# Attention scores from two 64-row products of halved fp32r operands, changed to one 99- or 102-row product of three bf16 parts

## The chip, the cores and the metric

One NeuronCore of a Trainium2 chip runs the whole program. The metric is device time in microseconds; lower is better. Times of the kernel before are three runs on one chip, and one further execution was recorded by the hardware profiler.

## What is computed

The reference is a stack of eight residual blocks on x[4, 512, 256]. Two of them are softmax attentions with 16 heads of 16 dimensions, and only these are touched:

```python
# block 1 (causal, with a bias that depends on head and key)
scores = einsum('bqhd,bkhd->bhqk', q, k) * scale + bias[None, :, None, :]
scores = where(causal, scores, -1e9)
p = softmax(scores, axis=-1); ctx = einsum('bhqk,bkhd->bqhd', p, v)
x = x + ctx @ Wout.T + b_out
# block 5 (no mask; rotary position on q and k; 4 key/value heads, repeated 4 times)
scores = einsum('bhqd,bhkd->bhqk', Qr, Kr) / HEAD_DIM ** 0.5
weights = softmax(scores, axis=-1); out = einsum('bhqk,bhkd->bhqd', weights, V_rep)
x = x + out @ W_o
```

The other six blocks are two expert feed-forwards, one attention over features, two sparse feed-forwards and a scan.

## The kernel before, in words

`stages` runs the blocks one behind the other. `attention` is called twice: "attn0" is block 1 (`causal` true), "attn1" is block 5. x stays in the on-chip memory for the whole program.

One attention has B = 4 sequences and 16 heads. Four heads make a unit, a unit has NT = 4 steps, one for each tile of 128 queries, so there are 64 steps, 16 for each sequence, and 15 more in which the pipeline empties or the last jobs run. The table `at` lists, for every step t, jobs for its middle and for its end. Each engine walks the same table, in the same order, and does the jobs that are its own. Nothing else orders the work: an engine goes through its list strictly in turn, and semaphores make it wait for the others.

A step has two halves of two heads each. In each half TensorE (PE) does, in this order:

- `scores1` (L940) of step t: the queries of one tile against keys, into banks 0 to 3 of PSUM, only for the row maxima. In attn0 the width is 128, 256, 384 or 512 keys for t mod 4 = 0, 1, 2, 3; in attn1 always 512.
- `scores2` (L964) of step t - 7: the transposed product, keys against queries, with the maxima as an extra row, into banks 4 and 5. Its widths in attn0 are 384, 256, 128, 512.
- in attn0 `masks1` (L950) and `masks2` (L973), which add the causal mask by products with an identity in bf16, 128 columns each.
- after the first half, the jobs of the step's middle.

After both halves come `context` (L988) of step t - 8, which multiplies probabilities with values for four heads side by side (128 rows, 32 columns, fp32), and the jobs of the step's end.

VectorE (DVE) takes the maximum over each half's scores (`row_max`, L1312), and ScalarE (ACT) the exponentials (L1160), one for each head. `scores1` of a half waits until the maximum of the half before last is taken, and `scores2` of a head waits until the exponential two heads earlier has emptied its bank.

**How a product of scores is made.** A number is cut into a high and a low fp32r part. A head's 16 dimensions are stacked three times (high·high, low·high, high·low), 48 rows; rows 48 and 49 carry the bias in attn0, row 63 the maximum, the rest are zeros. Heads lie in pairs: the even one in partitions 0 to 63 and the odd one in 64 to 127 of `qs` and `ks`, so that the two products of a half use the upper and the lower 64 rows of the array. `qs` and `ks` have two buffers, for alternating sequences.

**How the stacks are filled.** For each chunk (128 query or key rows, "q0", "k0", "q1", and in attn0 "k1") ACT writes the high part and DVE (attn0, and the first sequence of attn1) or GpSimd (POOL) the low part. Then SP's queue copies them into the stack, six DMAs a chunk (`stacks`, L828). Before the first of these the queue writes constants into the stacks: zeros (L850), ones (L843) and the bias (L868). The maxima of a unit go from `negm` through a PE transpose (L996, job `maxima`, in the middle of step 4u + 4) and an ACT copy to `mT`, and by two DMAs into the stack (L836). PE waits for them before step 4u + 7.

**Other jobs.** "rows" (L899) transposes the normalised x, "project" (L915) makes a chunk (in attn1 as "plain" in the middle and "swapped" at the end of a step), "values" (L928), "flip" (L1002) and "merge" (L1009) transpose results, "out" (L1018) is the last product. All of these and `maxima` use bank 7 (`MISC`), in the order of the table: PE may begin a job only when the job before it in that bank has been copied out by its engine. The first sequence's jobs ("early") run before step 0. After its early jobs DVE computes the norm statistics of the other three sequences (L119 to L1331), and only then takes the first row maximum.

## Time and profile before

| | us |
|---|---|
| median of three runs | 1644.63 (1636.43 to 1647.76) |
| profiled execution, its own time | 1641.78 |
| span of its trace | 1639.7 |
| attn0: first score product to last | 46.0 to 318 |
| attn1: first score product on | from 888.1 |

| engine | busy us (share) |
|---|---|
| PE | 1398.7 (85%) |
| PE weight loads | 1002.1 (61%) |
| DVE | 1049.0 (64%) |
| ACT | 625.2 (38%) |
| POOL | 295.8 (18%) |

The trace gives start and duration of each instruction, and for a gap the event that ended it. Ends of matmuls are modelled, so a busy PE is no proof of a PE at its limit; the distance between starts tells more. The engines run in turn through fixed lists, so the time of a stage is that of a chain that goes from engine to engine, and it is read from the starts.

### The profile page before, as it was taken

The page shows a single profiled execution, that of the slowest core. Times are in us where ns is not written, and L with a number is a line of the kernel's source. Part 1 is how long each engine was busy: PE and PEld are TensorE (multiplying, and loading weights), DVE is VectorE, ACT ScalarE, POOL GpSimd, SP SyncE. Part 2 cuts the span into 40 slices and gives each one's busy share as a digit, 9 for nine tenths or more (in the row PEclk, how much of TensorE's full clock was granted, in tenths as well). Part 3 has the DMA queues.
Part 4 walks back from the last instruction along what each step waited for, and adds up shares of the span by engine and source line. Part 5 has one row for each costly group of instructions (what it writes and reads, how often), then busy time and mean ns, then how long its engine had stood idle before and what let it go on. Part 6 is the DMA issues. An engine that isn't in the chain of part 4 may idle for free. (4 is left out here: it accounts for less than half of the span.)

```text
span 1639.7 us, 21649 instructions
## 1 busy us (share of the span) xinstructions
PE 1398.7 (85%) x8144; PEld 1002.1 (61%) x8144; DVE 1049.0 (64%) x2056; ACT 625.2 (38%) x1160; POOL 295.8 (18%) x251
## 2 busy tenths in 40 slices
PE   3799999857999877799976899898879979889897
PEld 2455555446888766688864444343257767677676
DVE  5555555187887456778746556666256568888775
ACT  1254544342333212333321455656632323433321
POOL 0210000044433200243331320200040200120010
PEclk9799999578999988999996799999989989999899
DMA  8615220040000000000015404110000000000000
GB/s 190 87 27 79 44 37 2 1 149 1 1 1 1 1 0 1 0 1 1 1 39 73 75 27 75 27 24 1 1 0 1 1 1 1 0 1 1 13 13 26
DMA packets 23063, 42.00 MB, mean 26 GB/s; under 512 B 4705, under 2 KB 6497, under 8 KB 22833
## 3 DMA queue, kind: packets, MB, share of 16 engines
q1 hardware_dynamic: 22960, 40.64, 13.2%
q8 instruction: 64, 1.05, 0.3%
q14 instruction: 39, 0.31, 0.1%
HBM read 14.54 MB, written 2.10 MB: 10 GB/s over the span
## 5 line engine op out<-in xcount | busy, mean ns | idle before, releaser
L1312 DVE TENSOR_REDUCE attn_negm<-ps 128x2 f32<-128x1024 f32 (+3 forms) x256 | 256.2, 1021 | 115.5 <-PE ps L940 57.4
L1160 ACT ACTIVATE attn_probs<-ps 128x512 f32<-128x512 f32 (+3 forms) x512 | 237.0, 515 | 188.9 <-PE ps L973 112.0
L480 POOL TENSOR_TENSOR moe_h_low<-moe_h,moe_h_high 128x512 fp32r<-128x512 f32 x96 | 139.8, 1458 | 328.8 <-ACT moe_h_high L430 328.8
L964 PE MATMUL ps<-attn_qs,attn_ks 64*128 64x512 f32 (+3 forms) x512 | 154.9, 418 | 38.1 <-ACT attn_probs L1160 35.4
L447 ACT ACTIVATE moe_silu<-ps 128x512 f32<-128x512 f32 x96 | 57.4, 598 | 228.0 <-PE ps L353 227.9
L940 PE MATMUL ps<-attn_ks,attn_qs 63*128 63x512 f32 (+3 forms) x512 | 120.9, 469 | 26.6 <-DMA attn_ks<-attn_part_low 21.5
L964 PEld LDWEIGHTS ps<-attn_qs,attn_ks 64*128 64x128 f32 x512 | 72.1, 193 | 102.7 <-ACT attn_probs L1160 97.9
L1683 PE MATMUL ps<-sb_f_down,tail_h 128*128 128x256 f32 x512 | 123.3, 387 | 7.1 <-DVEq L1976 7.1
L988 PE MATMUL ps<-attn_probs,attn_va 128*32 128x512 f32 (+3 forms) x1024 | 123.8, 559 | 0.0
L1683 PEld LDWEIGHTS ps<-sb_f_down,tail_h 128*128 128x128 f32 x512 | 98.5, 193 | 24.0 <-DVEq L1976 7.3
L940 PEld LDWEIGHTS ps<-attn_ks,attn_qs 63*128 63x128 f32 x512 | 51.9, 199 | 93.8 <-issue 62.4
L1949 DVE TENSOR_TENSOR tail_h<-tail_silu,ps 128x512 f32<-128x512 f32 x64 | 43.5, 682 | 89.0 <-PE ps L1673 56.9
L1789 ACT ACTIVATE tail_silu<-ps 128x512 f32<-128x512 f32 x64 | 38.1, 596 | 113.8 <-PE ps L1667 113.8
L503 DVE TENSOR_TENSOR moe_h<-moe_silu,ps 128x512 f32<-128x512 f32 x64 | 43.4, 686 | 56.7 <-PE ps L360 39.0
L382 PE MATMUL ps<-f_down_high,moe_h_high 128*128 128x256 f32 x256 | 73.9, 289 | 3.7 <-POOL moe_h_low L480 3.7
L382 PE MATMUL ps<-f_down_high,moe_h_low 128*128 128x256 f32 x256 | 72.6, 283 | 0.0
L382 PE MATMUL ps<-f_down_low,moe_h_high 128*128 128x256 f32 x256 | 72.1, 282 | 0.0
L430 ACT ACTIVATE moe_h_high<-moe_h 128x512 fp32r<-128x512 f32 x96 | 60.0, 625 | 29.7 <-DVE moe_h L503 29.1
L1667 PE MATMUL ps<-tail_xh,tail_gate_high 128*128 128x512 f32 x128 | 63.8, 498 | 2.9 <-POOL tail_up_low L1824 2.9
L1277 DVE RECIPROCAL attn_rden<-ps 128x16 f32<-128x16 f32 x32 | 8.2, 258 | 89.7 <-PE ps L1002 89.7
L1958 DVE TENSOR_TENSOR tail_ge<-tail_mag 128x1536 bf16<-128x1536 f32 (+2 forms) x48 | 55.8, 1218 | 0.7 <-ACT tail_mag L1777 0.7
L973 PE MATMUL ps<-sb_a_mask_kq,sb_identb 64*128 64x128 bf16 x512 | 52.8, 227 | 0.0
(319 smaller groups left out, 3281.2 us busy)
## 6 DMA issues: line engine op xcount, KB each, us to landing
attn_qs<-attn_part_high SPq DMA_DIRECT2D x64, 128.0 KB, 4.9
attn_qs<-attn_part_low SPq DMA_DIRECT2D x32, 128.0 KB, 4.5
attn_ks<-attn_part_high SPq DMA_DIRECT2D x32, 128.0 KB, 6.1
attn_ks<-attn_part_low SPq DMA_DIRECT2D x16, 128.0 KB, 7.0
out_x<-x SPq DMA_DIRECT2D x4, 512.0 KB, 2.6
x<-in_x SPq DMA_DIRECT2D x1, 1536.0 KB, 12.9
attn_qs<-attn_mT SPq DMA_DIRECT2D x64, 4.0 KB
moe_raw<-in_f_gate SPq DMA_DIRECT2D x2, 512.0 KB, 6.3
```

What stands on the lines that cost most here:

```text
L382: last = pe.matmul(ps[:, bank + t // 2, (t % 2) * D:(t % 2 + 1) * D], hp[:, j % RING, t * P:(t + 1) * P], wp[:, jw, :], start=j == 0 and t ...
L430: act.activation(hc.high[:, n % RING, :], h[:, n % RING, :], ACT.Copy).then_inc(high_done, 1)
L447: act.activation(sg[:, j % 2, :], ps[:, 2 * (j % 2), :], ACT.Silu).then_inc(silu_done, 1)
L480: pool.tensor_tensor(hc.low[:, j % RING, :], h[:, j % RING, :], hc.high[:, j % RING, :], ALU.subtract).then_inc(low_done, 1)
L940: last = pe.matmul(ps[:, 2 * (n % 2) + k, 0:width1(qt)], qs[e:e + ROWS1, b % 2, hd // 2, qt * P:(qt + 1) * P], ks[e:e + ROWS1, b % 2, key_ ...
L964: last = pe.matmul(ps[:, SC + k, 0:width2(kt)], ks[e:e + ROWS2, b % 2, key_tile(hd), kt * P:(kt + 1) * P], qs[e:e + ROWS2, b % 2, hd // 2, ...
L988: last = pe.matmul(ps[SLOT * j:SLOT * (j + 1), CTX, T - width2(kt):T], va[:, b % 2, kt, hd % KH, :], pr[:, s3 % RING, j, 0:width2(kt)], st ...
L1160: act.activation(pr[:, s2 % RING, j, 0:n], ps[:, SC + k, 0:n], ACT.Exp, scale=HD ** -0.5).then_inc(exp_done, 1)
L1312: dve.tensor_reduce(m, ps[:, 2 * half:2 * half + 2, 0:width1(qt)], AX, ALU.max, negate=True).then_inc(r1_free, 1)
L1667: last = pe.matmul(ps[:, bank, :], wp[:, c, j * P:(j + 1) * P], xp[:, p % 2, c, :], start=c == 0 and k == 0, stop=c == DC - 1 and k == 2)
L1683: last = pe.matmul(ps[:, DOWN + t // 2, (t % 2) * D:(t % 2 + 1) * D], h[:, j, t * P:(t + 1) * P], w_down[:, j, :], start=j == 0 and t % 2 ...
L1958: c.do(dve.tensor_tensor(ge[:, first:first + n, :], mag[:, lo, :].unsqueeze(1).broadcast_to([P, n, T]), mag[:, lo + 1:4, :], ALU.is_ge))
```

## The change

- The parts are bf16 and there are three of each number. A head has six products of 16 dimensions stacked (96 rows), then three rows of bias in attn0, then three rows of maximum: 99 or 96 rows for `scores1`, 102 or 99 for `scores2`. A head uses all 128 partitions; no two heads are paired. The number of score matmuls and their columns stay.
- A mask is one product over 128 rows where it was two over 64: two instructions for a half where there were four.
- No zero rows. Bias comes in three bf16 parts from the host.
- attn0: after DVE has taken the rest (`rest`, L1226 in the changed kernel), POOL makes parts two and three (L1161, L1163), and the copies wait for these. attn1: three subtractions or casts instead of one, on DVE for the first sequence (`low0`), on POOL for the others.
- The maxima are cut into three parts by four small DVE instructions (`split_maxima`, L1312 to L1315) behind the last `row_max` of a unit. PE turns the 48 columns in one bf16 product (L965), ACT copies 48 rows, one DMA loads them. The job moves from the middle of step 4u + 4 to that of 4u + 5.
- Each stack DMA moves as many bytes as before (128 KB), as 128 rows of 1 KB where it was 64 of 2 KB.

```diff
-DATA = 48
+DATA = 96
+PARTS = 3
...
-    MROW = P // 2 - 1
-    ROWS1, ROWS2 = MROW, MROW + 1
+    ROWS1 = DATA + (PARTS if causal else 0)
+    ROWS2 = ROWS1 + PARTS
...
-        at[4 * u + 4][0].insert(0, ("maxima", u))
+        at[4 * u + 5][0].insert(0, ("maxima", u))
...
-                if causal:
-                    sp.wait_ge(free["dve"], jobs.count[("project", b, ch, "plain")])
-                else:
-                    sp.wait_ge(low_ready, NCH * b + k + 1)
+                sp.wait_ge(low_ready, NCH * b + k + 1)
...
+                order = (0, 0, 1, 0, 1, 2) if ch[0] == "q" else (0, 1, 0, 2, 1, 0)
+                for r, which in enumerate(order):
+                    sp.dma_start(dst[16 * r:16 * r + 16, b % 2, first:first + n, :],
+                                 part[which][0:rows_of[ch], k, :]).then_inc(stack_loaded[int(ch[1])], 16)
...
-            zero_rows(ks)
-            zero_rows(qs)
-            ones_rows(ks, MROW, 1)
+            ones_rows(ks, ROWS1)
             if causal:
-                ones_rows(qs, DATA, 2)
-                sp.wait_ge(const_ready, 2)
+                ones_rows(qs, DATA)
+                sp.wait_ge(first_in, FIRST)
...
-                    e = 64 * k
-                    last = pe.matmul(ps[:, 2 * (n % 2) + k, 0:width1(qt)], qs[e:e + ROWS1, b % 2, hd // 2, qt * P:(qt + 1) * P],
-                                     ks[e:e + ROWS1, b % 2, key_tile(hd), 0:width1(qt)], start=True, stop=True)
+                    last = pe.matmul(ps[:, 2 * (n % 2) + k, 0:width1(qt)], qs[0:ROWS1, b % 2, hd, qt * P:(qt + 1) * P],
+                                     ks[0:ROWS1, b % 2, hd % KH, 0:width1(qt)], start=True, stop=True)
...
-                for c in range(2):
-                    for k in range(2):
-                        last = pe.matmul(ps[:, 2 * (n % 2) + k, qt * P:(qt + 1) * P], identb[64 * k:64 * k + 64, c, :],
-                                         w["mask_qk"][64 * k:64 * k + 64, c, :], start=False, stop=c == 1, skip_group_check=True)
-                        if c == 1:
-                            last.then_inc(r1_ready, 1)
+                for k in range(2):
+                    pe.matmul(ps[:, 2 * (n % 2) + k, qt * P:(qt + 1) * P], identb[:, :], w["mask_qk"][:, :],
+                              start=False, stop=True, skip_group_check=True).then_inc(r1_ready, 1)
...
+            def split_rest(b, ch):
+                k, n = CHUNKS.index(ch), rows_of[ch]
+                done = (1 if causal else 2) * (NCH * b + k + 1)
+                pool.tensor_copy(part[1][0:n, k, :], rest[0:n, k, :]).then_inc(rest_steps, 1)
+                pool.wait_ge(rest_steps, done)
+                pool.tensor_tensor(part[2][0:n, k, :], rest[0:n, k, :], part[1][0:n, k, :], ALU.subtract).then_inc(low_ready, 1)
...
+            def split_maxima(u):
+                if u >= 2:
+                    dve.wait_ge(ready, jobs.number[("maxima", u - 2)])
+                dve.wait_ge(r1_free, 2 * NT * (u + 1))
+                m, parts = negm[:, u % 2, :], mparts[:, u % 2, :]
+                cm.start(u)
+                cm.step(dve.tensor_copy(parts[:, 0:16], m))
+                cm.step(dve.tensor_tensor(mrest[:, :], m, parts[:, 0:16], ALU.subtract))
+                cm.step(dve.tensor_copy(parts[:, 16:32], mrest[:, :]))
+                dve.tensor_tensor(parts[:, 32:48], mrest[:, :], parts[:, 16:32], ALU.subtract).then_inc(m_split, 1)
```

**PE at the end of step 32 and the beginning of step 33 of attn1**, where a chunk of the last sequence is projected. Before (L940, L964 scores, L996 maxima, L988 context, L1002 flip, L915 the six products of a projection):

```order
L964 MATMUL ps<-attn_qs,attn_ks 128x512 x2
L996 MATMUL ps<-sb_ident,attn_negm 16x128
L940 MATMUL ps<-attn_ks,attn_qs 128x512 x2
L964 MATMUL ps<-attn_qs,attn_ks 128x512 x2
L988 MATMUL ps<-attn_probs,attn_va 32x512 x4
L1002 MATMUL ps<-sb_ident,attn_ctxs 128x128 x4
L940 MATMUL ps<-attn_ks,attn_qs 128x512 x2
L964 MATMUL ps<-attn_qs,attn_ks 128x512 x2
L915 MATMUL ps<-attn_xh,attn_wq_high 128x512
```

And now, from the first half of step 33 on (L916, L936 scores, L965 maxima, L892 projection, L957 context):

```order
L916 MATMUL ps<-attn_ks,attn_qs 128x512 x2
L936 MATMUL ps<-attn_qs,attn_ks 128x512 x2
L965 MATMUL ps<-sb_identb,attn_mparts 48x128
L892 MATMUL ps<-attn_xh,attn_wq_high 128x512
L892 MATMUL ps<-attn_xl,attn_wq_high 128x512
L892 MATMUL ps<-attn_xh,attn_wq_low 128x512
```

The maxima stood a step earlier, with a flip between them and the projection; now they stand directly ahead of the projection, and both use bank 7.

**SP's queue ahead of the first stack copies of attn0.** Before:

```order
L856 DMA x<-in_x 128x3072
L850 DMA attn_ks<-attn_zeros 13x8x512 x4
L850 DMA attn_qs<-attn_zeros 13x8x512 x4
L843 DMA attn_ks<-attn_ones 1x8x512 x4
L843 DMA attn_qs<-attn_ones 2x8x512 x4
L868 DMA attn_ks<-attn_bias_high 1x8x512 x4
L868 DMA attn_ks<-attn_bias_low 1x8x512 x4
```

Now:

```order
L837 DMA x<-in_x 128x3072
L832 DMA attn_ks<-attn_ones 3x16x512 x2
L832 DMA attn_qs<-attn_ones 3x16x512 x2
L845 DMA attn_ks<-sb_a_bias 1x16x512 x6
L821 DMA attn_qs<-attn_part 16x8x512 x6
L821 DMA attn_ks<-attn_part 16x8x512 x6
```

Twenty-four copies of constants become ten, and the eight of zeros, 208 KB each, are gone.

## Rows read from the trace of the kernel before

**Rows 1.** Waits, 46 to 331 us (attn0): engine line, awaited; us in total, times, longest.

```profile
ACT attn_probs L1160 <- PE ps L973: 112.0, 112, 3.3
...
PEld ps L964 <- ACT attn_probs L1160: 36.0, 84, 1.2
```

**Rows 2.** Busy time by stretch: start:end, length, busy (x count), PEclk, DMA share, GB/s.

```profile
46.00:102.00 56.00, 49.59 (x438) 30.80 (x438) 32.26 (x43) 20.00 (x48) 7.57 (x8) 0.83 0.48 68
```

**Rows 3.** Timeline, step 61 of attn1: start, us, engine, line, xcount, [idle before, releaser].

```profile
1152.30 0.50 PE L940 MATMUL ps<-attn_ks,attn_qs 63*128 63x512 f32 x2
1152.64 0.40 PE L964 MATMUL ps<-attn_qs,attn_ks 64*128 64x512 f32 x2
1153.13 1.08 ACT L1160 ACTIVATE attn_probs<-ps 128x512 f32<-128x512 f32 x2 [1.64 <-PE ps L964]
1153.78 0.98 PE L964 MATMUL ps<-attn_qs,attn_ks 64*128 64x512 f32 x2 [0.51 <-ACT attn_probs L1160]
...
1154.70 1.07 PE L988 MATMUL ps<-attn_probs,attn_va 128*32 128x512 f32 x8
1155.69 0.49 PE L940 MATMUL ps<-attn_ks,attn_qs 63*128 63x512 f32 x2
```

**Rows 4.** Timeline, step 55 of attn0, second half.

```profile
258.52 0.18 PEld L964 LDWEIGHTS ps<-attn_qs,attn_ks 64*128 64x128 f32 x1 [0.31 <-ACT attn_probs L1160]
258.52 0.11 PEld L950 LDWEIGHTS ps<-sb_a_mask_qk,sb_identb 64*128 64x128 bf16 x2
...
259.31 0.60 ACT L1160 ACTIVATE attn_probs<-ps 128x512 f32<-128x512 f32 x1 [0.84 <-PE ps L973]
```

**Rows 5.** Timeline, the beginning of attn0.

```profile
7.31 4.67 SPq L850 DMA_DIRECT2D attn_ks<-attn_zeros  x4
...
19.74 0.63 ACT L1148 ACTIVATE attn_wv_high<-sb_a_wv 128x512 fp32r<-128x512 f32 x1 [10.95 <-DMA x<-in_x]
...
24.38 2.64 SPq L868 DMA_DIRECT2D attn_ks<-attn_bias_low  x4
...
34.25 4.00 DVE L119 BATCH_NORM_STATS2 attn_stats<-x 128x6 f32<-128x256 f32 x12
...
41.69 0.17 DVE L130 SCALAR_TENSOR_TENSOR attn_rstd<-attn_newton,attn_rstd 128x12 f32<-128x12 f32 x1
41.89 0.17 DVE L1331 TENSOR_SCALAR attn_minus<-attn_mv 128x12 f32<-128x12 f32 x1
...
46.03 0.47 PE L940 MATMUL ps<-attn_ks,attn_qs 63*128 63x128 f32 x2 [12.43 <-DMA attn_ks<-attn_part_low]
```

**Rows 6.** The page's DMA issues over the program: count, KB each, us to landing.

```profile
attn_qs<-attn_part_high SPq DMA_DIRECT2D x64, 128.0 KB, 4.9
...
x<-in_x SPq DMA_DIRECT2D x1, 1536.0 KB, 12.9
```

**Rows 7.** Timeline, the beginning of attn1.

```profile
880.45 0.69 DVE L1269 TENSOR_TENSOR attn_part_low<-attn_qk,attn_part_high 128x512 fp32r<-128x512 f32 x1 [0.70 <-ACT attn_part_high L1096]
881.05 4.00 DVE L119 BATCH_NORM_STATS2 attn_stats<-x 128x6 f32<-128x256 f32 x12
...
888.94 1.23 DVE L1312 TENSOR_REDUCE attn_negm<-ps 128x2 f32<-128x1024 f32 x1 [0.16 <-PE ps L940]
```

**Rows 8.** Timeline, a projection's last product in attn1 and the scores behind it.

```profile
1035.63 0.40 PE L915 MATMUL ps<-attn_xh,attn_wq_low 128*128 128x512 f32 x1
1035.95 0.19 PEld L940 LDWEIGHTS ps<-attn_ks,attn_qs 63*128 63x128 f32 x2 [0.36 <-issue]
```

**Rows 9.** Timeline, step 8 of attn0: maxima, their copy, a projection.

```profile
71.22 0.27 PE L996 MATMUL ps<-sb_ident,attn_negm 128*16 128x128 f32 x1
71.85 0.25 ACT L1111 ACTIVATE attn_mT<-ps 16x128 fp32r<-16x128 f32 x1
...
72.20 0.59 PE L915 MATMUL ps<-attn_xh,attn_wk_high 128*128 128x512 f32 x1 [0.71 <-ACT attn_mT L1111]
```

**Rows 10.** Timeline, one subtraction on POOL in attn1.

```profile
1049.61 1.27 POOL L1187 TENSOR_TENSOR attn_part_low<-attn_qk,attn_part_high 128x512 fp32r<-128x512 f32 x1
```

More of the change, by code:

```diff
@@ L754, in attention @@
         cut = {n: Halves(s.sb(n + "_high", w[n].shape, F32R), s.sb(n + "_low", w[n].shape, F32R)) for n in names}
-        part = Halves(s.sb("part_high", [P, NCH, T], F32R), s.sb("part_low", [P, NCH, T], F32R))
-        qs, ks = s.sb("qs", [P, 2, HEADS // 2, T], F32R), s.sb("ks", [P, 2, KT, T], F32R)
-        ones = s.sb("ones", [HEADS, T], F32R)
-        zeros = s.sb("zeros", [P, T], F32R)
-        if causal:
-            bias = Halves(s.sb("bias_high", [HEADS, T], F32R), s.sb("bias_low", [HEADS, T], F32R))
-        else:
+        part = [s.sb(f"part{r}", [P, NCH, T], BF16) for r in range(PARTS)]
+        qs, ks = s.sb("qs", [P, 2, HEADS, T], BF16), s.sb("ks", [P, 2, KH, T], BF16)
+        ones = s.sb("ones", [PARTS * HEADS, T], BF16)
+        rest = s.sb("rest", [P, NCH, T])
+        if not causal:
             qk, rot = s.sb("qk", [P, NCH, T]), s.sb("rot", [P, 2, T])
@@ L1084, in project @@
                     act.wait_ge(ready, jobs.number[job])
-                    act.activation(part.high[0:n, k, :], ps[0:n, jobs.bank[job], :], ACT.Identity,
+                    act.activation(part[0][0:n, k, :], ps[0:n, jobs.bank[job], :], ACT.Identity,
                                    bias=w["bqk"][0:n, k:k + 1]).then_inc(high_ready, 1)
@@ L1095, in high @@
                 act.wait_ge(turned, NCH * b + k + 1)
-                act.activation(part.high[0:n, k, :], qk[0:n, k, :], ACT.Copy).then_inc(high_ready, 1)
+                act.activation(part[0][0:n, k, :], qk[0:n, k, :], ACT.Copy).then_inc(high_ready, 1)
             def values(b, v):
@@ L1205, in _ @@
                     turn(0, job[2])
+                if causal and job[0] == "project":
+                    projected(0, job[2])
             normalise(1)
@@ L1214, in _ @@
                             turn(job[1], job[2])
+                        if causal and job[0] == "project":
+                            projected(job[1], job[2])
                         if job[0] == "high":
@@ L1335, in _ @@
                         row_max(2 * t + half)
+                        if half == 1 and t % NT == NT - 1:
+                            split_maxima(t // NT)
                     for job in todo:
@@ L2091, in bf16_bits, with bf16_parts @@
     return (bits >> 16).astype(np.uint16)
[L2094 to L2096 removed]
 def head_rows(heads):
[L2101 removed]
+    return np.array([HD * h + d for d in range(HD) for h in range(heads)])
+def bf16_parts(v):
+    parts = []
+    for _ in range(PARTS):
+        parts.append(bf16_bits(v))
+        v = v - (parts[-1].astype(np.uint32) << 16).view(np.float32)
+    return np.concatenate(parts)
 def shape_constants():
```

133 lines of the change are left out of this document (56 added, 77 removed).

## The prediction

> **What bounds the kernel now.** I read the views in this order. The busy shares do not decide: PE is busy 85%, but with modelled ends. The chain that ended last lies in the last third, which the change leaves alone; so I read the two attentions for themselves: their waits first, then the timeline of single steps, then the place where each attention begins.
>
> The waits of attn0 name no single full engine: ACT waits 112.0 us for PE's masks, and PE's weight loads wait 36.0 us for ACT's exponentials [rows 1]. The two wait for each other in turn; what counts is the length of that ring. One plain step of attn1 shows it [rows 3]: scores1 at 1152.30, scores2 at 1152.64, its two exponentials from 1153.13 to 1154.21, the second half's scores2 from 1153.78, because head by head they wait for these exponentials, then the context at 1154.70, and the next step at 1155.69. The step is 3.39 us. Of it the first half's products up to the first exponential are 0.83, the exponentials and the loads behind them 1.1, the second half's last product until the context 0.4, the context 0.99. The second half's scores1 lies beside the exponentials and costs nothing. In attn0 the same ring holds the masks too [rows 4]: the second head's weight load starts at 258.52, the next exponential at 259.31, 0.79 us later.
>
> What begins attn0 is a transfer: PE's first score product waits until 46.03 for the copies into the stack, 12.43 us after its last early product [rows 5]. Ahead of the stack copies SP's queue issues constants until 27.02, and the early projections themselves start late, because ACT waits for x's 1.5 MB until 19.74 [rows 5]. DVE is close behind as the bound: its statistics run from 34.25 to 42.06. In attn1 DVE is the bound at the beginning: statistics from 881.05, first maximum at 888.94 [rows 7].
>
> **The change, part by part.** The sum is made against the profiled execution, 1641.78 us.
>
> *Products in turn.* Before, two heads' products share a slot: 0.34 us from the first pair to the next, 0.11 of it exposed weight load and 0.23 the 512 columns [rows 3]. Now two heads stand one behind the other. For bf16 columns I take the same 0.23 at most; four of 512 columns take 0.05 + 4 x 0.22 = 0.93 where two pairs took 0.57. The first exponential needs only the third of the four, so it starts 0.15 later. The load for bf16 weights is shorter: two masks' loads fit in 0.11 where one fp32r load takes 0.18 [rows 4]. That gives back 0.05 on the last product of the second half. So a step of attn1 gets 0.09 longer, 64 x 0.09 = **+5.8**. In attn0 one mask of 128 rows takes the slot of a pair of 64, and where the heads are apart (second half) four masks stand in the ring and not eight: the 0.79 of rows 4 become about 0.65. The 16 steps with 512 columns in both products (t mod 4 = 3) gain this and lose 0.22 in front: +0.1 each. The 48 narrower ones lose little in front: -0.1 each. Together 1.6 - 4.8 = **-3.2**. The seven emptying steps of each attention have no scores1 and gain 0.1: **-1.5**.
>
> *No switch between 64 and 128 rows.* After a projection of 128 rows the next scores1 loads its weights 0.32 us after the start of the last product, whose 512 columns take 0.23: 0.09 of a gap, and the load's 0.11 is exposed [rows 8]. With all in 128 rows both should go. Jobs at a step's end: 16 flips, 8 merges, 8 outs, 6 rows in each attention and 9 swapped projections in attn1, 85 in all, each with one switch on the ring: 85 x 0.2 = **-17**. The context, 32 columns wide, still switches twice a step.
>
> *Steps that wait for nothing.* In 12 steps of attn1 and 18 of attn0 a projection or a values job stands in the middle; the exponentials are over when PE returns, and every column counts. Attn1: four pairs x 0.22 = 0.88 more, less two switches of 0.2 and 0.1 of loads, about +0.35; attn0, with 320 columns in the mean, +0.1: **+6**.
>
> *Maxima a step later.* Directly ahead of a projection in the same bank, they make PE wait until ACT has copied them, and ACT does this behind the half's two exponentials. The one place that has this order now is step 8 of attn0: product at 71.22, copy at 71.85, projection at 72.20, 0.71 us waited [rows 9]. In the new order this is so in steps 5, 17, 21, 33, 37 of attn0 and 5, 17, 33 of attn1; in the two steps 5 ACT has no exponentials yet. From rows 3 the wait would be 1.4 in attn1 (exponentials end 1.9 into the step, the copy takes 0.25, PE is there at 0.9). I take 1.0 x 6, less 1.0 for step 8: **+5**. For the deadline, step 4u + 7, more than one step of 2.4 us or longer is left after the copy, and one DMA of this kind takes under 2.
>
> *DVE's four small instructions.* 0.20 from start to start [rows 5], 0.85 a unit. They lie between the last maximum of a unit and the next step's first, where DVE waits anyway. In the first steps, where DVE is the bound, they count: **+0.9** in attn1, **+0.5** in attn0.
>
> *Beginning of attn0.* Eight copies of zeros (1.66 MB) and six others go. I assume that x then lands 4.7 us earlier: 512 KB take 2.6 us to write, 1536 KB would take 8 by that, and take 12.9 beside the zeros [rows 6]. All early work moves with it, DVE's statistics end at 37.4. The stack copies lose the wait for SP's queue and gain two POOL instructions, 1.27 us each by the nearest row [rows 10]; by that the twelve copies that step 0 needs are issued by 32 and landed, at 4.9 us each [rows 6], by 38. Taken: **-8**. Bounds: -11, if nothing but x counts, and 0, if landing is unchanged.
>
> *Beginning of attn1.* DVE makes three parts instead of two for three chunks: a cast (0.4) and a subtraction of 0.69 [rows 7] with two waits, 1.25 each, all ahead of the statistics: +3.8, less 0.5 for the memset of zeros: **+3.3**. Other POOL work (the same cuts for later sequences) has 16 steps of cover, 50 us for 5 us.
>
> Sum: 5.8 - 3.2 - 1.5 - 17 + 6 + 5 + 1.4 - 8 + 3.3 = -8.2, so 1633.6. The median of three stands 2.9 above the profiled execution, so on its scale 1636. I forecast **1635**.
>
> **Rivals.** *A, faster, 1620.* In 46 to 102 us PE's clock was granted at 0.83 [rows 2], that is 19 us at 1.2 GHz and the rest at 2.4 GHz, behind the long wait. With a shorter wait and more columns in flight it may stay high: half of these 19 us, and the same again in attn1's first stretch. 15 us in the best case, under 1635. Against it: the wait before step 0 does not vanish, and PE had waits of this kind before.
>
> *B, slower, 1665.* PE becomes the bound. 256 pairs of 512 columns (0.23) and 256 of 320 in the mean (0.14) are 59 + 36 = 95 us of streaming that comes on top, and my sum exposes only 12. It decides as soon as the second half's scores1 ends after the first exponential: by rows 3 at 1.38 against 1.58 us into the step, 0.2 of margin. If every step goes over and a third is exposed, +32. For it: the margin is small, and in attn0 the narrow exponentials leave less. Against it: the ring has 1.1 us of exponentials in each step. The Trainium skill (TensorEngine Tiling (Array Packing), Theoretical Speedup) gives products of at most 64 rows up to a doubling by tiles, which this change gives up; by that rule alone all 95 would show and the time be 1730. Rows 3 speak against: PE's score products wait for ACT there.
>
> *C, the copies, 1645.* A copy is now 128 rows of 1 KB. If the time goes by rows and not by bytes, the twelve copies ahead of step 0 take twice as long (19 instead of 9.6 us at one each 0.8, 46 - 27 us for 24), the beginning of attn0 gains nothing (+8), and that of attn1 loses some us more. No row has 1 KB between on-chip places. The Trainium skill (DMA: Bandwidth & Descriptors, Specifications) puts the minimum for full rate at 512 B; by it C would be out, and no row here shows it.
>
> *D, no effect of the missing switch, 1648.* If the 0.2 of rows 8 belongs to the scores' first load in any mode, -17 shrinks to -4.
>
> **How the numbers follow.** Forecast 0.50, A 0.20, B 0.10, C 0.10, D 0.10. About 1% (16.4 us) is what a measurement of this kernel can tell from no change. Faster by more, under 1628.2: A nearly whole and the lower edge of the forecast, 0.27. Slower by more, over 1661.1: B's larger part, 0.08. Within: 0.65. The range 1619 to 1650 takes in A's centre, C and D, and leaves B and A's far side out.
>
> **What would show it.** Right: the first score product of attn0 at 36 to 40 us; plain steps of attn1 3.45 to 3.5 us apart; scores right behind a flip with no gap; steps 17 and 33 longer by 0.5 to 1.4 us; attn1's first maximum about 3.5 us later behind its block's beginning. Wrong: PE's weight loads of scores2 no longer waiting for exponentials (B); the first product still at 44 or later (C); PE's clock at 1.0 throughout (A).

## The result, and the profile after

| | before | after | ratio of after to before |
|---|---|---|---|
| median of four runs of each, us | 1643.55 | 1624.41 (1616.93 to 1629.84) | 0.9857 [0.9813, 0.9902] |
| once more, six runs of the change, us | 1643.61 | 1622.26 | 0.986 [0.9822, 0.9898] |
| profiled execution, span, us | 1639.7 | 1617.3 | |
| second profile of each, span, us | 1645.2 | 1616.9 | |

The change is 1.4% faster, inside the forecast's range and beyond its 1%. The kernel's time varies with the clock that PE is granted, and one profile is not enough for that, so both kernels were profiled twice. The table gives the stages, each from one start of a PE product to the next ("loop": from the first product of `scores1` to the last; "emptying": from there to the last product of `out`; the last products of `scores2` lie in it):

| stage, us | before | before, 2nd | after | after, 2nd | mean change |
|---|---|---|---|---|---|
| up to attn0's first score product | 46.0 | 44.3 | 40.1 | 41.0 | -4.6 |
| loop of attn0 | 241.3 | 251.7 | 236.5 | 236.0 | -10.3 |
| emptying of attn0 | 43.4 | 43.5 | 32.5 | 31.9 | -11.3 |
| from there to attn1's first score product | 557.3 | 552.4 | 553.0 | 552.8 | -2.0 |
| loop of attn1 | 271.6 | 272.5 | 277.2 | 277.1 | +5.1 |
| the rest | 480.0 | 480.8 | 478.1 | 478.2 | -2.2 |

The profiles differ by 25.3 us, the medians by only 19 and 21. Of the 25.3 us, 4.7 lie in stages of other blocks, which the change leaves alone (2.2 in the last row, 2.5 between attn0 and the beginning of attn1).

attn1, which shares all the products' changes, got slower. The gain lies in attn0's loop and emptying. The table by stretches says why. Its columns are start:end, length, busy time (x count) of PE, PE's weight loads, DVE, ACT and POOL, then PE's granted clock, DMA share and GB/s. Before, first profile (attn0's loop, its emptying, attn1's loop):

```profile
46.03:287.31 241.28, 222.88 (x2188) 133.56 (x2189) 129.74 (x182) 109.05 (x276) 12.04 (x12) 0.94 0.31 43
287.31:330.80 43.49, 35.90 (x213) 18.30 (x207) 5.19 (x9) 15.04 (x38) 0.00 (x0) 0.61 0.00 1
888.10:1159.70 271.60, 243.35 (x1265) 107.69 (x1265) 170.56 (x178) 149.39 (x286) 40.65 (x39) 0.94 0.21 37
```

Before, second profile, attn0's loop and emptying:

```profile
44.30:296.00 251.70, 234.65 (x2189) 140.15 (x2189) 129.81 (x182) 109.04 (x276) 13.20 (x12) 0.88 0.29 42
296.00:339.50 43.50, 35.77 (x212) 18.32 (x205) 5.19 (x9) 15.15 (x38) 0.00 (x0) 0.61 0.00 1
```

After, the same three stretches:

```profile
40.11:276.60 236.49, 214.35 (x1709) 123.05 (x1709) 143.07 (x243) 108.99 (x277) 34.93 (x37) 0.96 0.36 49
276.60:309.10 32.50, 24.47 (x173) 11.68 (x171) 5.75 (x13) 15.15 (x38) 0.00 (x0) 0.89 0.01 1
862.10:1139.20 277.10, 254.32 (x1264) 98.35 (x1265) 187.79 (x253) 149.04 (x287) 55.41 (x57) 0.94 0.22 36
```

The clock has two levels, 1.2 and 2.4 GHz, so a stretch of length L at a granted clock c spent 2 x (1 - c) x L at the lower one. In attn0's loop that is, summed unrounded, 29.8 and 61.1 us before, 17.1 and 12.4 after; in the emptying 34.1 and 34.1 before, 6.8 and 3.4 after. The two profiles of before give the price: 10.4 us more for 31.3 us more at 1.2 GHz, **0.33 us for each us at the lower clock**, with the same instructions. (Between the runs over 65 and 96 rows below it is 12.4 us for 31.0, or 0.40.) In the changed kernel no stretch at 1.2 GHz lies between 60 and 280 us, in either profile; before had 3 in the first profile (72, 134, 202 us) and 5 in the second (71 to 273 us).

The steps can also be compared directly. Where a step ran wholly at 2.4 GHz in a profile of each kernel, its shortest times are set side by side: 54 of the 63 steps of attn0's loop are together 0.6 us longer after the change, 53 of attn1's 1.3 us longer. So the instructions gained nothing in the sum.

The single step has hardly changed. Timeline of step 61 of attn1 after (start, us, engine, line, xcount, [idle before, releaser]), to be laid beside [rows 3]:

```profile
1131.39 0.60 PE L916 MATMUL ps<-attn_ks,attn_qs 96*128 96x512 bf16 x2
...
1131.83 0.59 PE L936 MATMUL ps<-attn_qs,attn_ks 99*128 99x512 bf16 x2
...
1132.30 1.09 ACT L1127 ACTIVATE attn_probs<-ps 128x512 f32<-128x512 f32 x2 [1.63 <-PE ps L936]
...
1133.44 0.10 PEld L936 LDWEIGHTS ps<-attn_qs,attn_ks 99*128 99x128 bf16 x1 [0.39 <-ACT attn_probs L1127]
...
1134.76 0.39 PE L916 MATMUL ps<-attn_ks,attn_qs 96*128 96x512 bf16 x1
```

The first exponential comes 0.91 us into the step (before 0.83), and from the last `scores2` to the next step it is 1.32 us (before 1.42): 3.37 us for 3.39. Steps with a flip went from 3.98 to 3.87, those with a projection in the middle from 5.66 to 5.87 and 7.16 to 7.37. In attn0 the widest steps (t mod 4 = 3) grew from 3.22 to 3.35 and plain narrow ones fell from 2.40 to 2.34. So the ring of PE and ACT is the same one; PE's weight loads still wait for the exponentials (after, 40 to 309 us of the trace, to be compared with [rows 1]):

```profile
ACT attn_probs L1127 <- PE ps L944: 100.0, 110, 3.1
PEld ps L936 <- ACT attn_probs L1127: 43.4, 100, 0.9
```

What got longer is the step with the maxima right ahead of a projection. Step 33 of attn1, 8.57 us, before 7.13:

```profile
1011.50 1.09 ACT L1127 ACTIVATE attn_probs<-ps 128x512 f32<-128x512 f32 x2 [1.64 <-PE ps L936]
...
1011.57 0.24 PE L965 MATMUL ps<-sb_identb,attn_mparts 128*48 128x128 bf16 x1
1012.47 0.26 ACT L1080 ACTIVATE attn_mT<-ps 48x128 bf16<-48x128 f32 x1
...
1012.83 0.47 PE L892 MATMUL ps<-attn_xh,attn_wq_high 128*128 128x512 f32 x1 [1.03 <-issue]
...
1014.06 0.40 PE L892 MATMUL ps<-attn_xh,attn_wq_low 128*128 128x512 f32 x1
1014.30 0.12 PEld L916 LDWEIGHTS ps<-attn_ks,attn_qs 96*128 96x128 bf16 x2 [0.27 <-issue]
```

PE stands for 1.03 us until ACT, behind two exponentials, has emptied the bank. The last two rows answer to [rows 8]: the load now comes 0.24 us after the product's start, not 0.32.

One more wait grew, at the beginning of step 11 of attn1, where PE needs the second unit's maxima. Before:

```profile
934.00 0.19 PEld L940 LDWEIGHTS ps<-attn_ks,attn_qs 63*128 63x128 f32 x2 [3.34 <-DMA attn_qs<-attn_mT]
```

After:

```profile
904.11 3.73 SPq L821 DMA_DIRECT2D attn_ks<-attn_part  x6
...
908.53 0.78 SPq L827 DMA_DIRECT2D attn_qs<-attn_mT  x1
...
912.46 0.13 PEld L916 LDWEIGHTS ps<-attn_ks,attn_qs 96*128 96x128 bf16 x2 [5.65 <-DMA attn_qs<-attn_mT]
```

PE turned these maxima at 899.4, but their DMA stands in SP's queue behind stack copies and is issued at 908.53. Step 10 takes 10.71 and 10.42 us, before 8.19 and 8.34; with POOL's instructions shortened and the maxima a step earlier (e6_short_pool below) it takes 7.56. Two steps later PE runs at the higher clock where before it did not, so steps 10 to 13 together grew by only 0.3 to 0.5 us.

The beginning of attn0, to be compared with [rows 5]:

```profile
16.53 0.63 ACT L1115 ACTIVATE attn_wv_high<-sb_a_wv 128x512 fp32r<-128x512 f32 x1 [8.37 <-DMA x<-in_x]
...
25.62 3.83 SPq L821 DMA_DIRECT2D attn_qs<-attn_part  x6
...
37.80 0.17 DVE L1331 TENSOR_SCALAR attn_minus<-attn_mv 128x12 f32<-128x12 f32 x1
...
40.12 0.37 PE L916 MATMUL ps<-attn_ks,attn_qs 99*128 99x128 bf16 x2 [10.53 <-DMA attn_ks<-attn_part]
```

x lands at 16.5 (before 19.7), the copies are issued from 25.6 (before 27.1), and yet PE waits until 40.1. The DMA view tells why: packets, MB and rate while the stacks are filled, after (28 to 40 us) and before (30 to 39 us).

```profile
DMA packets 1749, 1.59 MB, mean 133 GB/s; under 512 B 193, under 2 KB 1749, under 8 KB 1749
```

```profile
DMA packets 930, 1.51 MB, mean 168 GB/s; under 512 B 193, under 2 KB 193, under 8 KB 930
```

All 16 DMA engines are busy in both. In these two stretches a packet of 1 KB takes 0.134 us in the mean where one of 2 KB took 0.201: the copies land 1.01 us apart, before 0.86. Yet before waited longer, because its last signal came late: eleven of the twelve copies were there at 39.3 us, the last one only at 45.9.

The beginning of attn1, against [rows 7]:

```profile
856.34 0.43 DVE L1257 CAST attn_part<-attn_rest 128x512 bf16<-128x512 f32 x1
856.80 0.69 DVE L1259 TENSOR_TENSOR attn_part<-attn_rest,attn_part 128x512 bf16<-128x512 f32 x1
857.41 4.01 DVE L119 BATCH_NORM_STATS2 attn_stats<-x 128x6 f32<-128x256 f32 x12
...
865.06 2.35 DVE L1302 TENSOR_REDUCE attn_negm<-ps 128x2 f32<-128x1024 f32 x2
```

From the last product of the block ahead to the first maximum it is 40.7 us, before 38.7 and 37.4. To the first score product it is 37.7, before 37.9 and 36.5: most of this loss lies inside the "loop of attn1", whose step 0 takes 4.3 us in place of 2.1, because DVE comes later to its first maximum.

### The profile page after: what moved, and what is told of

Read it like the earlier page. It is cut to its first block and busy times, and to the rows that moved or that the text cites. A ratio compares the mean times of both kernels' runs of the same rounds, so it can differ in the third digit from the quotient of the medians.

```text
span 1617.3 us, 20802 instructions
## 1 busy us (share of the span) xinstructions
PE 1384.7 (86%) x7632; PEld 970.3 (60%) x7632; DVE 1073.8 (66%) x2187; ACT 623.9 (39%) x1159; POOL 346.3 (21%) x301
## 5 line engine op out<-in xcount | busy, mean ns | idle before, releaser
L936 PE MATMUL ps<-attn_qs,attn_ks 99*128 99x512 bf16 (+4 forms) x512 | 153.6, 347 | 30.7 <-ACT attn_probs L1127 18.9
L916 PE MATMUL ps<-attn_ks,attn_qs 96*128 96x512 bf16 (+4 forms) x512 | 142.4, 362 | 31.0 <-DMA attn_ks<-attn_part 20.9
L936 PEld LDWEIGHTS ps<-attn_qs,attn_ks 102*128 102x128 bf16 (+1 forms) x512 | 49.1, 97 | 126.9 <-ACT attn_probs L1127 100.5
L957 PE MATMUL ps<-attn_probs,attn_va 128*32 128x512 f32 (+3 forms) x1024 | 118.3, 535 | 0.0
L916 PEld LDWEIGHTS ps<-attn_ks,attn_qs 99*128 99x128 bf16 (+1 forms) x512 | 40.1, 101 | 91.6 <-issue 46.8
L503 DVE TENSOR_TENSOR moe_h<-moe_silu,ps 128x512 f32<-128x512 f32 x64 | 43.4, 687 | 60.3 <-PE ps L360 39.6
L1669 PE MATMUL ps<-tail_xl,tail_gate_high 128*128 128x512 f32 x128 | 52.5, 410 | 0.0
```

Source lines behind the costliest of these rows:

```text
L916: last = pe.matmul(ps[:, 2 * (n % 2) + k, 0:width1(qt)], qs[0:ROWS1, b % 2, hd, qt * P:(qt + 1) * P], ks[0:ROWS1, b % 2, hd % KH, 0:width1 ...
L936: last = pe.matmul(ps[:, SC + k, 0:width2(kt)], ks[0:ROWS2, b % 2, hd % KH, kt * P:(kt + 1) * P], qs[0:ROWS2, b % 2, hd, T - width2(kt):T] ...
L957: last = pe.matmul(ps[SLOT * j:SLOT * (j + 1), CTX, T - width2(kt):T], va[:, b % 2, kt, hd % KH, :], pr[:, s3 % RING, j, 0:width2(kt)], st ...
L1669: last = pe.matmul(ps[:, bank, :], wp[:, c, j * P:(j + 1) * P], xp[:, p % 2, c, :], start=c == 0 and k == 0, stop=c == DC - 1 and k == 2)
```

## The experiments

**Does the clock's place belong to the kernel?** Second profiles of both (before2 and after2, unchanged code).

> The kernel before once more, for a second profile. Theory: stretches at 1.2 GHz again in steps 8, 24, 25 and 40 of attn0 (72, 134 and 202 us) and while attn0 empties (304 to 328 us). Rival 'chance': other places, and the emptying of attn0 at full clock, so that most of the 10.5 us that it saved in the profiles is no part of the change's worth.

> The changed kernel once more, for a closer ratio and a second profile. Theory 'clock by the work in hand': the stretches at 1.2 GHz come at the same places as in its first profile (33 to 57, 289 to 296, 313 to 330 us, nothing between 60 and 285). Rival 'chance': others, with some between 60 and 285 us. Ratio to the kernel before 0.984 to 0.990.

Measured: after2 1622.26 us, before2 1647.16 in its one run; the stages stand above. The places of the kernel before differed between its profiles (only about 72 and 200 us came back), but it had 3 and 5 stretches within 60 to 280 us, the change none; and the emptying was at 1.2 GHz for 34 us both times. "Chance" is right for the single place and wrong for the sum: the whole-program clock was 0.909 to 0.930 in all runs of the kernel before, and 0.931 to 0.942 in all ten of the change.

**What giving up the pairs costs** (e1_serial).

```diff
-                    e = 64 * k
+                    e = 0
...
-  identb[64 * k:64 * k + 64, c, :], w["mask_qk"][64 * k:64 * k + 64, c, :]
+  identb[0:64, c, :], w["mask_qk"][0:64, c, :]
```

> The kernel before, in which both heads of a pair use rows 0 to 63 of the array (and the masks too), so that their products stand one behind the other as in the change; nothing else differs (the odd head's scores are those of the even one). It tells what giving up the pairs costs by itself, and what it does to PE's clock. My forecast's step: an attn1 plain step grows from 3.39 to 3.5 us, attn0 by a few us, in all about +10, ratio 1.006. Theory 'clock' (more columns in flight keep PE's clock high in attn0 and in its emptying steps): the half-clock stretches of the kernel before at 72, 134, 202 and 304 to 328 us are gone, and the time is equal or lower than before, ratio 0.99 to 1.00. Rival 'PE bound': plain steps of 3.7 us or more, ratio over 1.015.

Measured: 1766.58 us, ratio 1.0709 [1.0639, 1.078], far from every theory. A plain step of attn1 takes 3.61 us (with 3.39 before), so there the steps' own part is 64 x 0.22 = 14 us of 120. In attn0, where the masks stand in turn too, a plain narrow step at full clock takes 3.08 us for 2.40, and the 27 steps that run at full clock in both kernels are 0.81 longer in the mean; for all 63 that would be 51 us, an estimate. attn0's loop took 337 us, PE was busy 332 of them, and the granted clock was 0.76. So the theory "clock" falls: more columns in flight did not keep the clock up. The rival "PE bound" is out for attn1, whose step stays under its 3.7, and fits attn0.

**The 64-row mode and the rows** (e3_rows64, e9_rows65, e10_rows96): the changed kernel's score products over fewer rows of the same stacks, the columns unchanged.

```diff
-  qs[0:ROWS1, b % 2, hd, ...], ks[0:ROWS1, b % 2, hd % KH, ...]
+  qs[0:64, b % 2, hd, ...], ks[0:64, b % 2, hd % KH, ...]     (65, 96; scores2 likewise)
```

All three leave bias and maxima out of the scores, and the first two other parts of the sum as well.

> The changed kernel with score products over 64 rows of the stacks only (the rest of the sum, bias and maxima are left out of the scores), so that scores are in 64-row mode again, one head behind the other; all else is the same. It isolates the switch between 64 and 128 rows. If the switch costs 0.2 us a time: flip steps of attn1 4.07 and plain ones 3.38, outs 5.4, in all some 10 to 17 us more than the changed kernel. If it costs nothing and the gain came from shorter weight loads: the same time within 3 us. Clock: if it goes by columns, the clock's stretches are those of the changed kernel; if by rows in use, they are those of the kernel before.

> As e3_rows64, with one row more: products over 65 rows, so that the array is in 128-row mode while hardly more rows are in use. Against e3_rows64 (1669 us; attn0's loop 272.2 us, 76.8 of it at half clock; flip steps of attn1 3.96) it tells whether the mode or the rows in use made that time. Theory 'mode': no switches, flip steps 3.87, and attn0's loop 236 us with 10 to 20 us at half clock, as in the changed kernel; time 1622 to 1628. Theory 'rows in use': flip steps 3.87 too, but attn0's loop keeps 40 to 70 us at half clock and takes 245 to 260 us; time 1635 to 1655.

> Control for the two runs over 64 and 65 rows, whose scores lack bias and maximum so that the exponentials overflow: products over rows 0 to 95, that lack the same, with nearly all rows of the change in use. If those values have no part in it, time and clock are the changed kernel's: 1618 to 1628 us, attn0's loop 236 us with 10 to 20 us at half clock. If the values themselves move the clock, it stands near e3_rows64 or e9_rows65 instead.

| rows | median us | ratio to before | attn0's loop us | its clock | flip step of attn1 |
|---|---|---|---|---|---|
| 64 | 1669.45 | 1.0146 [1.0107, 1.0186] | 272.3 | 0.86 | 3.96 |
| 65 | 1642.29 | 0.9973 [0.9937, 1.0009] | 248.7 | 0.90 | 3.87 |
| 96 | 1624.66 | 0.9854 [0.9779, 0.993] | 236.3 | 0.96 | 3.87 |
| 99 and 102 (after2) | 1622.26 | 0.986 [0.9822, 0.9898] | 236.0 | 0.97 | 3.87 |

The rows by stretches of e3_rows64, attn0's loop and attn1's:

```profile
41.50:313.80 272.30, 257.91 (x1709) 121.23 (x1709) 145.21 (x243) 109.76 (x277) 35.72 (x38) 0.86 0.31 42
...
902.70:1191.10 288.40, 267.50 (x1265) 98.04 (x1265) 188.02 (x255) 148.96 (x287) 55.34 (x57) 0.91 0.22 35
```

e9_rows65:

```profile
40.80:289.50 248.70, 227.36 (x1708) 128.81 (x1709) 143.27 (x243) 108.95 (x276) 35.30 (x37) 0.90 0.34 46
...
880.60:1162.10 281.50, 258.68 (x1265) 99.72 (x1265) 187.86 (x254) 149.06 (x287) 55.41 (x57) 0.93 0.22 35
```

e10_rows96:

```profile
41.10:277.40 236.30, 214.31 (x1709) 123.08 (x1709) 143.00 (x243) 108.97 (x277) 35.21 (x37) 0.96 0.36 49
```

From 65 to 96 rows the steps that run at full clock do not differ (plain 3.37 and 3.38, flip 3.87, step 17 of attn1 8.57 in both; 97 steps of the two loops together 0.4 us), so the 17.6 us between the medians go by the clock. The clock of a stage comes from one profile each, and the two profiles of before alone lay as far apart (29.8 and 61.1 us at 1.2 GHz) as these two (48.6 and 17.6). What carries the reading is that all runs agree: ten over 65 rows took 1636 to 1650 us at whole-program clocks of 0.915 to 0.927, four over 96 rows 1620 to 1631 at 0.934 to 0.938. So the theory "rows in use" forecast e9_rows65 rightly.

From 64 to 65 rows more than the rows changes. The masks of the change use 128 rows, so over 64 rows every step of attn0 has changes of mode between scores and masks. That fits its plain narrow step, 2.54 us at full clock, over 65 rows 2.33. e3_rows64 came out 45 to 47 us above the change and not 10 to 17, and its stretches at 1.2 GHz are neither those of the change nor those of before: 76.9 us in attn0's loop.

The run over 96 rows lacks bias and maxima like the other two and has the change's time, so their absence plays no part. This is the central result: at equal columns, the granted clock of attn0's loop was 0.90 with 65 rows and 0.96 with 96; over 64 rows, with the switches besides, it was 0.86.

The switch itself is read at full clock, from a flip's first product to the scores behind it. e3_rows64:

```profile
1182.64 0.66 PE L971 MATMUL ps<-sb_ident,attn_ctxs 128*128 128x128 f32 x4
...
1183.22 0.11 PEld L916 LDWEIGHTS ps<-attn_ks,attn_qs 64*128 64x128 bf16 x2 [0.17 <-issue]
1183.22 0.60 PE L916 MATMUL ps<-attn_ks,attn_qs 64*128 64x512 bf16 x2
```

The changed kernel, a flip of the same sequence:

```profile
1112.78 0.66 PE L971 MATMUL ps<-sb_ident,attn_ctxs 128*128 128x128 f32 x4
...
1113.17 0.21 PEld L916 LDWEIGHTS ps<-attn_ks,attn_qs 96*128 96x128 bf16 x2
1113.28 0.60 PE L916 MATMUL ps<-attn_ks,attn_qs 96*128 96x512 bf16 x2
```

0.58 us against 0.50; the whole flip step is 0.09 longer. Steps of attn1 with a projection in the middle, two switches, were 0.19 to 0.28 longer over 64 rows than over 65. A switch on the chain costs 0.09 to 0.14 us. The Trainium skill (TensorEngine Tiling (Array Packing), Tiling Modes) says that a change of mode drains the engine; the trace shows the delay, at this price, and not the draining itself.

**The emptying by the clock alone** (e8_filled_tail): the kernel before, with PE given work there.

```diff
+                if s1 == STEPS:
+                    pe.wait_ge(r1_free, 2 * STEPS)
...
+                    elif s2 < STEPS:
+                        filler(half)      # scores1 of the last step again, two products, unread
```

> The kernel before, with scores1's products of the last step issued again, unread, in the seven emptying steps of each attention, so that PE has in them the products of a full step. The emptying of attn0 took 43.4 and 43.5 us in the two profiles, 34.1 us of it at half clock; in the changed kernel 31.9 to 32.5 with 3.4 to 6.8. If the clock alone makes that difference, the filled emptying has under 15 us at half clock and takes 34 to 38 us, attn1's stays, 5 to 9 us less than the kernel before. Rival: the change's emptying steps are shorter by themselves (no switch, other products): the clock stays high, but 40 us or more remain; or the added products only lengthen the steps.

```profile
289.00:324.50 35.50, 29.36 (x240) 15.30 (x235) 5.18 (x9) 15.15 (x38) 0.00 (x0) 0.95 0.00 1
```

The emptying of attn0 fell from 43.5 to 35.5 us with added work, at a clock of 0.95: the clock makes at least 8 of the 11.3 us. At 0.37 us for each us at 1.2 GHz (worked out below) the emptying of before would take 32 us at the change's clock, so the remaining 3 are more likely the filler's own cost; no run separates them. The 11.3 us themselves are at the upper end of what the change gives. The emptying took 32.1 us in e4_zeros, but 36.3 in e10_rows96 and 35.5 to 38.4 in the four versions that moved the job of the last maxima, which lies in it (e2, e5, e6, e7), with 12 to 24 us at 1.2 GHz. The whole was 1647.9 us, ratio 1.0018 [0.9984, 1.0052]: the 8 us don't show. In the profile the stages outside attn0 were longer by 2 to 7 us up to attn1 and by 3 behind its loop, where the filler also runs; what of it the filler causes wasn't separated.

**The place of the maxima** (e2_maxima4, e5_mixed, e6_short_pool).

```diff
-        at[4 * u + 5][0].insert(0, ("maxima", u))
+        at[4 * u + 4][0].insert(0, ("maxima", u))                       # e2, e6
+        at[4 * u + (4 if u % 4 == 3 else 5)][0].insert(0, ("maxima", u))   # e5
```

> The changed kernel with the job maxima back in the middle of step 4u + 4. If the later place makes PE wait for ACT's copy ahead of a projection (as I forecast), steps 17, 33 of attn1 fall from 8.57 to about 7.2 us and steps 5, 17, 33 of attn0 by 0.8 each, but step 8 of each gets its old wait back: 4 to 6 us less than the changed kernel in all. Rival: the longer path over DVE's four small instructions makes PE wait at 4u + 4 for the parts, and every fourth step grows by 0.3 to 0.8 us: 30 units, 10 us more.

Measured: 1631.57 us, ratio 0.9875 [0.9811, 0.994], in its profile 14.6 us longer than the change's. Steps 17 and 33 of attn1 fell to 7.35 and 7.33, those of attn0 to 4.77, as forecast. But steps 8, 20 and 36 of attn0 rose from 6.17, 4.40 and 4.40 to 11.99, 7.38 and 6.97, and PE's clock fell at each (69, 120, 188 us), which it did not in the change. attn0's loop is 9 us longer than the change's and its emptying 5 to 6. Its timeline at step 8:

```profile
65.94 2.34 POOL L1182 TENSOR_TENSOR x<-x,sb_a_bo 128x1024 f32<-128x1024 f32 x1
66.17 2.13 DVE L1312 CAST attn_mparts<-attn_negm 128x16 bf16<-128x16 f32 x1
...
68.91 1.17 POOL L1163 TENSOR_TENSOR attn_part<-attn_rest,attn_part 128x512 bf16<-128x512 f32 x1
69.10 1.01 DVE L1315 TENSOR_TENSOR attn_mparts<-attn_mrest,attn_mparts 128x16 bf16<-128x16 f32 x1
...
70.25 0.27 PE L965 MATMUL ps<-sb_identb,attn_mparts 128*48 128x128 bf16 x1 [4.05 <-DVE attn_mparts L1315]
```

DVE's instructions on 16 columns, 0.17 us elsewhere, last until POOL's instruction ends (68.28 and 68.30; 70.08 and 70.11). In the changed kernel they do so too (2.16 us at 65.58), but there PE asks for the parts a step later. So the rival of this run, in a form that neither theory had, is right.

> As e2_maxima4 (the changed kernel with the job maxima at 4u + 4), but POOL's two instructions a chunk that make parts two and three work on 8 of 512 columns (the scores lack most of these parts). In e2_maxima4 DVE's small instructions at steps 8 and 20 ended just when POOL's ended (2.16 us beside the 2.34 us of L1182, 0.80 beside L1163, alone 0.17). If they are locked out by POOL's work: step 20 falls from 7.4 to about 4.5 us, step 8 keeps the 2.2 us beside L1182 but loses the later ones, attn0's first score product comes 1 to 2 us earlier. Rival: DVE's length there has another cause, steps 8 and 20 stay at 12 and 7 us.

```diff
-                pool.tensor_copy(part[1][0:n, k, :], rest[0:n, k, :])
+                pool.tensor_copy(part[1][0:n, k, 0:8], rest[0:n, k, 0:8])     (the subtraction likewise)
```

Measured: 1623.28 us, ratio 0.9865 [0.9817, 0.9914]. Step 20 fell from 7.38 to 4.78, step 8 from 11.99 to 8.75. Step 36 still took 6.09, with no DVE instruction held and 2.9 us of it at 1.2 GHz. At step 8 what is left of the hold is again POOL's biased add:

```profile
63.96 2.35 POOL L1186 TENSOR_TENSOR x<-x,sb_a_bo 128x1024 f32<-128x1024 f32 x1
...
65.58 0.75 DVE L1316 CAST attn_mparts<-attn_negm 128x16 bf16<-128x16 f32 x1
```

The cast begins 1.6 us into the add and ends with it (66.33 and 66.31). The first score product came 0.6 us earlier than in e2, not 1 to 2; PE still waits 9.5 us there for the copies (in e2_maxima4 10.3). The Trainium skill (SBUF — State Buffer, SBUF: two separate sides) describes an exclusive lock of a port pair that DVE and GpSimd share, by which the later one waits for the whole instruction; the trace agrees.

> The changed kernel with the job maxima back in the middle of step 4u + 4 for the last unit of each sequence alone (there no projection and no work of POOL is near), and at 4u + 5 for the others. Steps 17, 33 of attn0 go from 5.53 to 4.77 us, those of attn1 from 8.57 to 7.35, steps 16, 32, 48 get 0.1 to 0.2 longer; steps 8, 20, 36 of attn0 stay as in the changed kernel. 3 to 4 us less than the changed kernel, ratio to it 0.998. Rival: PE's clock falls somewhere else for it and the gain isn't seen.

Measured: 1618.01 us, ratio 0.9835 [0.9798, 0.9873], against 1622.26 for after2 on the same chip: 4.2 us less, as forecast. In the profile attn1's loop is 2.3 us shorter (274.8), attn0's 0.5 to 1.0, but the emptying of attn0 is 3 us longer, and the span, 1617.0, is no shorter than the change's. The intervals of the two ratios overlap. What is sure is that steps 17 and 33 take 4.78 us (attn0) and 7.33 (attn1) in place of 5.53 and 8.57. Its median is the lowest here.

**The zeros** (e4_zeros).

```diff
+            if causal:
...
+                            sp.dma_start(dst[102 + 13 * part_:115 + 13 * part_, buf, :, :],
+                                         zeros[0:104, :].unsqueeze(1).broadcast_to([104, 2, T])).then_inc(const_loaded, 16)
```

These are eight DMAs of 208 KB, into rows 102 to 127 of `ks` and `qs`.

> The changed kernel with attn0's eight fills of 208 KB of zeros issued again at the same place, into rows 102 to 127 that nobody reads (in pieces of 1 KB, before it was 2 KB). My forecast says that they cost the beginning: x lands at 19 to 20 instead of 16.5 us, the first score product comes 4 to 8 us later than 40.1, the time grows by 4 to 8 us. Rival: the beginning is bound by the stack copies alone (12 at 1.02 us), which start later only if x does, and the straggling last copy of the kernel before has another cause: first score product under 42.

Measured: 1628.52 us, ratio 0.9876 [0.9813, 0.994], 4 to 6 us above the change. x lands at 19.9, the first score product is at 46.76, 5.7 to 6.6 us later; attn0's loop is 234.6. The fills account for the whole gain at the beginning. They also bring back the late signal, which answers this run's rival: eleven copies are there at 42.2 us and the last at 46.6.

**PE kept at work in the waits** (e7_warm): e5_mixed with 36 unread products ahead of each step 0.

```diff
+            for k in range(36):
+                pe.matmul(ps[:, k % 2, :], cut["wq"].high[:, 0, 0:P], xT.high[:, 0, :], start=True, stop=True)
```

> e5_mixed, and in each attention 36 products of 128 rows and 512 columns into banks 0 and 1, which nobody reads, between the early jobs and step 0, where PE otherwise waits 10.8 us for the copies into the stacks. They compute nothing of the result. At full clock they take 36 x 0.22 = 8 us and fit into the wait. If PE's idleness there is why the first steps of both attentions run at 1.2 GHz (33 to 57 and 852 to 883 us), both stretches get shorter by 10 to 20 us; in the loops a us at half clock cost 0.33 us (before and its second profile: 29.8 and 61.1 us at half clock, 241.3 and 251.7 us long), so 6 to 12 us less than e5_mixed, ratio to it 0.993 to 0.996. Rival: the clock falls all the same, or falls later in the loop; then no gain, and at half clock the 36 take 15.5 us, 4 to 5 us too long, twice: 8 us more.

Measured: 1621.92 us, ratio 0.9869 [0.9843, 0.9896], 3.9 us above e5_mixed. The stretch at 1.2 GHz moved from 33 to 57 us to 44 to 58, in attn1 the 31 us from 852 became three short ones. But the loops gained only 0.6 and 0.5 us for 2.9 and 7.6 us less at 1.2 GHz, and attn1's step 0 began 3.9 us later in its block. In attn1 steps 0 and 1 got 2.4 us shorter and steps 5 and 10 lost 1.7 of it again; step 10 ends in the wait for the maxima's DMA. A higher clock is worth little where PE waits for something else.

## Why the prediction was right, and where it was not

The time lies in the range, a third of the way from A's 1620 to the forecast's 1635. The sign was right, but the step "the sum" was not what made it, and for the sum that is luck: at equal clock the change is worth about nothing. The clock, which the sum left out and only rival A had (held at 0.20, and at 15 us "in the best case"), made some 21 of the profiles' 25 us. That is an estimate: in the mean 30.7 us less at 1.2 GHz in attn0's loop at 0.33, and 29 us less in its emptying at 0.37, the slope between e10_rows96's emptying, 36.3 us with 17.1 at 1.2 GHz, and after's, 32.5 with 6.8. At the other slope, 0.40, the loop's part would be 2 us more. A was not right about the place either. From 46 to 102 us before had 19.6 us at 1.2 GHz, and the first stretch of the change's loop still has 17.1 and 12.4; what vanished lies later in the loop and in the emptying.

What is left in the parts that the change touches: -4.6 at the beginning of attn0, -0.1 in its loop, -0.6 in its emptying, +0.5 up to attn1's first score product and +5.1 in its loop, together +0.3, where I had -8.2. The rest of the 25 us, 4.7, lies in other blocks.

- *Products in turn.* Forecast +0.09 a step of attn1, measured -0.01 to -0.02. The front was mis-sized (+0.08, not +0.15) and the end (-0.10, not -0.05). At 64 rows and bf16 a plain step is 3.37 too, with fp32r in turn 3.61 (e1_serial): the format paid for the pairs, 0.24 a step, which I had at 0.05.
- *No switch.* -17 is -8 to -12: 0.09 to 0.14 for each of the 85. The rows that I took 0.2 from [rows 8] held a load that is exposed in both modes. D's -4 is about as near as the forecast.
- *Steps that wait for nothing.* Forecast +0.35, measured +0.19 to +0.22 in attn1, where a projection or values job stands in the middle and no maxima are ahead of it.
- *Maxima a step later.* Forecast 1.0 x 6 less 1.0. Measured 1.24 in attn1 (7.33 in e5_mixed against 8.57) and 0.75 to 0.87 in attn0, about +5.7. Right. Step 8, forecast at -1.0, gave about -0.2 (6.41 at full clock in e8_filled_tail, 6.17 after). What this step of the forecast did not see is what the place avoids: e2_maxima4 is 7 to 9 us slower. And "for the deadline" it counted one DMA of under 2 us from the copy; at step 11 of attn1 that DMA was held up in SP's queue, and PE waited 5.65 us where it had waited 3.34.
- *DVE's four small instructions.* Forecast 0.85 a unit; so it is in 26 of 32 units. In 6 POOL holds one or more, at step 8 of attn0 for 3.9 us in all. In the changed kernel the step is none the longer for it, since PE asks for the parts a step later. No row of before had such an instruction beside POOL, and I looked for none.
- *Beginning of attn0.* Forecast -8, measured -5.9 and -3.3. x came 3.2 us earlier, not 4.7; the copies land 1.01 us apart, before 0.86. What the sum did not see is that before waited for a late last signal. Had that come 0.86 us behind the eleventh copy, before's first product would have stood at 40.1 in its first profile, as the change's does (an estimate); e4_zeros shows that the signal is late only with the fills. C is half right: time goes neither by rows nor by bytes, but 1 KB pieces move 133 GB/s where 2 KB moved 168. The Trainium skill (DMA: Bandwidth & Descriptors, Specifications), by which 512 B would do, does not hold for these copies; the measurement decides.
- *Beginning of attn1.* Forecast +3.3 and +0.9, measured +2.0 to +3.3. Right.
- *B, slower.* Excluded: PE's loads still wait for the exponentials. As a warning it had substance: the same columns over 64 rows, with more switches, gave 1669 us, more than its 1665, and in e1_serial PE was busy 332 of 337 us of attn0's loop.

A's own reason, more columns in flight, fell with e1_serial and e3_rows64, which have the change's columns and lower clocks than before. What stays open is why the kernel before, which used 126 to 128 rows by pairs for half the time, stood between 65 and 96 rows (in the mean of its profiles 45 us at 1.2 GHz in attn0's loop, against 49 and 18); that was not tried apart from the columns. The format (fp32r or bf16) and the number of mask products changed as well, and only the rows were varied alone, so what part each of them has in the clock of before is not shown.

## What to carry to other kernels

Compare the granted clock stage by stage and in two profiles before giving a gain to the instructions: here the steps at full clock add up to nearly the same time, and some 20 us come from where the clock was. Before moving a job in a fixed order look at both sides: the bank or engine that it now stands ahead of, and what runs beside its producer where it stood. Small DVE instructions on the chain belong where POOL is idle. A small transfer that the chain waits for should not stand in a queue behind large ones.

## What the runs showed of the hardware that was not expected

- At equal columns, 64, 65 and 96 rows in the score products gave clocks of 0.86, 0.90 and 0.96 in attn0's loop, and 1669, 1642 and 1625 us in all; with 64 the switches of mode come on top.
- A us at 1.2 GHz cost 0.33 to 0.40 us in attn0's loop; in e7_warm 7.6 us less of it at the beginning of attn1 gave 0.5.
- A DVE cast of 16 columns took 2.16 us beside a POOL add, for 0.17 alone.
- Copies within the on-chip memory in pieces of 1 KB ran at 133 GB/s, of 2 KB at 168, all DMA engines busy in both.
- In the kernel before the last of the stack copies' 192 signals came at 45.9 and 44.2 us. In the first profile the 176th was there at 39.3; after, the last came at 40.0, 1.0 behind the 176th. With the eight fills of zeros put back (e4_zeros) it came at 46.6, 4.4 behind.
